# Layer 2's weights quantised and stored beside the convolution, and the first pair's layer 1 put between the weight chunks

## The reference, cut to what matters

```python
x = x + tanh(g_xattn[0]) * long_conv(ctx, ctx, layernorm(x), ssm_kernel, D, 8)
x = x + tanh(g_ffn[0]) * ffn(layernorm(x), ln_w, ln_b, W1, b1, W2, b2)

# long_conv, per head of 8 rows (64 heads, 1024 steps, batch 8)
kv  = einsum('bhil,bhjl->bijhl', k, v)                # k = v = ctx
y   = irfft(rfft(kv, 2L) * rfft(ssm_kernel, 2L))[:L]  # a causal convolution
out = einsum('bijhl,bhil->bjhl', y + kv * D, q)       # q = layernorm(x)

# ffn, on 4096 rows of 1024; hidden width 4096
h = bf16(layernorm(bf16(x)) * ln_w + ln_b)
h = bf16(mx_quant(h) @ mx_quant(W1).T + b1)
h = bf16(gelu(h))
h = bf16(mx_quant(h) @ mx_quant(W2).T + b2)
return bf16(bf16(x) + h)
# mx_quant: per block of 32 along the contraction, a power of two from the block's
# largest magnitude; round(x / scale), clipped to -128..127, times scale
```

## Time and profile before

| what | value |
|---|---|
| median of 3 runs | 2108.7 us (2106.93 to 2108.92) |
| the profiled execution | 2109.22 us |
| its span in the profile | 2107.4 us |
| PE busy | 1936.4 us (92%) |
| DVE busy | 1713.9 us (81%) |
| POOL busy | 915.4 us (43%) |
| ACT busy | 736.8 us (35%) |
| mixer block | about 0 to 1027 us |
| preparation of the weights | about 1027 to 1180 us |
| groups of tiles | about 1180 to 2107 us |

### The profile page before, as it was taken

One profiled execution on the slowest core, in us unless ns is written; L12 is line 12 of the kernel. 1 busy time (PEld: TensorE's weight loads), 2 busy tenths in 40 slices (PEclk: granted clock), 3 DMA queues, 4 the chain that ended last, 5 costly groups with the idle time before them and its releaser, 6 DMA issues.

```text
span 2107.4 us, 29465 instructions
## 1 busy us (share of the span) xinstructions
PE 1936.4 (92%) x11776; PEld 1493.9 (71%) x11776; DVE 1713.9 (81%) x2091; ACT 736.8 (35%) x1028; POOL 915.4 (43%) x1036
## 2 busy tenths in 40 slices
PE   6999999999999999999232579999999999999998
PEld 5888888888888888888231456666666666666663
DVE  6888788888888878887799888888888898888844
ACT  3222222222222222222141444444444444545440
POOL 4888888888888888888501000000000000000000
PEclk9999999999999999999655789999999999999999
DMA  5445445444544544542568201111111111111111
GB/s 196 147 163 183 151 156 176 163 143 170 172 149 155 182 159 153 171 153 98 188 213 280 78 21 61 61 61 45 55 53 60 61 61 41 51 61 61 41 41 70
DMA packets 61160, 247.62 MB, mean 117 GB/s; under 512 B 7200, under 2 KB 7200, under 8 KB 52832
## 3 DMA queue, kind: packets, MB, share of 16 engines
q1 hardware_dynamic: 61024, 245.74, 34.0%
HBM read 211.57 MB, written 34.14 MB: 117 GB/s over the span
## 4 chain that ended last, share of the span: by engine, by line
PE 43%; DVE 7%; issue 1%; DMA 0%; ACT 0%; POOL 0%; DVEq 0%; POOLq 0%; ACTq 0%
PE acc_ps L670 21%; PE l_ps L655 21%; DVE arena L915 2%; DVE f_o_res L915 2%; DVE w_T L930 1%; DVE arena L930 1%; PE tr_ps L633 1%; DMA arena<-in_w 0%; DVE f_stats L782 0%; DVE f_stats L781 0%; DVE arena L881 0%; DVE arena L891 0%; DVE f_amax_x L826 0%; DVE f_o_res L920 0%; DVE arena L920 0%
## 5 line engine op out<-in xcount | busy, mean ns | idle before, releaser
L217 PE MATMUL y_ps<-kk_hi,slab 128*128 128x512 f32 (+8 forms) x3072 | 870.6, 366 | 5.3 <-DMA slab<-taps_scratch 5.3
L217 PEld LDWEIGHTS y_ps<-kk_hi,slab 128*128 128x128 f32 x3072 | 557.7, 188 | 101.5 <-DMA slab<-taps_scratch 5.7
L217 PE MATMUL y_ps<-kk_lo,slab 128*128 128x512 f32 (+8 forms) x1536 | 561.9, 366 | 0.0
L655 PE MATMUL l_ps<-f_xq_T,w_T 128*128 128x256 bf16 x4096 | 457.7, 275 | 68.4 <-ACT arena L735 66.1
L655 PEld LDWEIGHTS l_ps<-f_xq_T,w_T 128*128 128x128 bf16 x4096 | 403.6, 99 | 123.2 <-ACT arena L735 66.7
L670 PE MATMUL acc_ps<-w_T,arena 128*128 128x512 bf16 x2048 | 449.0, 379 | 0.0
L670 PEld LDWEIGHTS acc_ps<-w_T,arena 128*128 128x128 bf16 x2048 | 198.8, 98 | 232.2
L991 POOL TENSOR_TENSOR f_rstd<-f_var_eps,f_neg_half 128x1 f32<-128x1 f32 x32 | 21.8, 682 | 741.9 <-DVE f_var_eps L794 741.9
L217 PEld LDWEIGHTS y_ps<-kk_lo,slab 128*128 128x128 f32 x1536 | 289.8, 189 | 47.5
L735 ACT ACTIVATE arena<-l_ps,f_b 128x256 bf16<-128x256 f32 x512 | 213.7, 471 | 279.8 <-PE l_ps L655 221.9
L453 POOL TENSOR_TENSOR lsum<-lower 128x240 f32<-128x240 f32 (+1 forms) x128 | 254.8, 1991 | 122.8 <-DVE lower L359 122.8
(11 more groups left out here) (101 smaller groups left out, 1954.1 us busy)
## 6 DMA issues: line engine op xcount, KB each, us to landing
slab<-taps_scratch SPq DMA_DIRECT2D x128, 512.0 KB, 4.4
arena<-in_w_m SPq DMA_DIRECT2D x32, 1024.0 KB, 6.9
arena<-x_scratch SPq DMA_DIRECT2D x64, 512.0 KB, 3.9
arena<-in_w SPq DMA_DIRECT2D x32, 1024.0 KB, 4.9
k_ext<-in_ctx_e SPq DMA_DIRECT2D x64, 384.0 KB, 3.0
x_tile<-in_x_t SPq DMA_DIRECT2D x32, 512.0 KB, 4.7
x_scratch<-x SPq DMA_DIRECT2D x32, 512.0 KB, 2.9
out_t<-arena SPq DMA_DIRECT2D x32, 512.0 KB, 2.6
```

The costliest lines, as they stand in the source:

```text
L217: mm = nc.tensor.matmul(y_ps[:, y_base + begin:y_base + end], slab[s][:, half, d * P:(d + 1) * P], kk_part[s][:, begin - d * PAIR:end - d ...
L655: mm = nc.tensor.matmul(l1_ps[bank % L1_BANKS][:, a, :], w1_T[:, k, col:col + P], xq_T[:, k, :], start=(k == 0), stop=(k == L // P - 1))
```

## The change

W2 gets its own layout (`w2_t`), a scratch tensor in HBM (`w2_q`, 16 chunks of 512 KB in bf16), and is quantised in the mixer block. There DVE takes the weight maxima on each of the first 32 heads (one a head, not one in two), makes all scales on head 32, and from head 32 on runs `layer2_ints` on each even head and `layer2_clip` and `layer2_quant` on each odd one. SP loads a maxima chunk on each of the first heads, and in the second half loads a chunk of W2 and stores a quantised one in each tile. In the feed-forward block the preparation has only W1's 16 chunks; SP loads the finished W2 after them. Tiles 0 and 1 are prepared before chunk 0 is finished, and PE runs bank j-1 of the first group's layer 1 after it has turned chunk j; ACT adds the biases and applies gelu in the same loop, DVE takes two of the four peaks and the statistics of tiles 2 and 3 in it. The wait quoted above is gone, since `hidden[0]` no longer lies in buffers of the raw weights (two of them are in `w2_T` now). The scales of W1 are made in half the width.

```diff
@@ mixer_block, sync
+            def load_w2(j):
+                if j >= 2:
+                    sp.wait_ge(w2_stored, 16 * (j - 1))
+                sp.dma_start(w2_raw[j % 2], w2_t[j]).then_inc(w2_loaded, 16)
+            def store_w2(j):
+                sp.wait_ge(w2_quant, j + 1)
+                sp.dma_start(w2_q[j], w2_raw[j % 2][:, 0:L].bitcast(BF16)).then_inc(w2_stored, 16)
...
-                    if t + 1 < tiles:
-                        sp.wait_ge(w_max_ready, t)
-                        load_w(t + 1)
+                if 1 <= h < tiles - 1:
+                    sp.wait_ge(w_max_ready, h)
+                    load_w(h + 1)
+                if h in (tiles - 2, tiles - 1):
+                    load_w2(h - (tiles - 2))
+                if t > half:
+                    if h % TILE_HEADS == 0:
+                        store_w2(t - half - 1)
+                    elif t + 1 < tiles:
+                        load_w2(t - half + 1)
...
             first_loads(sp)
+            store_w2(tiles - half - 1)
             store_x1(tiles - 1)
+            sp.wait_ge(w2_stored, 16 * (tiles - half))
@@ mixer_block, vector
+            def layer2_ints(j):
+                dve.wait_ge(w2_loaded, 16 * (j + 1))
+                if j == 0:
+                    dve.wait_ge(w_inv_ready, 2)
+                else:
+                    dve.wait_ge(w2_quant, j)
+                nc.vector.tensor_tensor(w2_int.rearrange("p (c o) -> p c o", o=L), w2_raw[j % 2].rearrange("p (c o) -> p c o", o=L),
+                                        view(w_inv, L, [(0, 2), (1, L)]), ALU.mult).then_inc(w2_ints, 1)
+            def layer2_clip(j):
+                dve.wait_ge(w2_ints, j + 1)
+                nc.vector.tensor_scalar(w2_int, w2_int, 127.0, None, ALU.min).then_inc(w2_clipped, 1)
+            def layer2_quant(j):
+                w2_scale_twice = view(w2_scale, 0, [(0, 2), (1, L)])
+                dve.wait_ge(w2_clipped, j + 1)
+                nc.vector.tensor_tensor(w2_raw[j % 2][:, 0:L].bitcast(BF16).rearrange("p (c o) -> p c o", o=L),
+                                        w2_int.rearrange("p (c o) -> p c o", o=L),
+                                        w2_scale_twice, ALU.mult).then_inc(w2_quant, 1)
...
-                if h % TILE_HEADS == 1:
-                    weight_maxima(t)
+                if h < tiles:
+                    weight_maxima(h)
+                if h == tiles:
+                    weight_scales()
+                if t >= half:
+                    if h % TILE_HEADS == 0:
+                        layer2_ints(t - half)
+                    else:
+                        layer2_clip(t - half)
+                        layer2_quant(t - half)
             times_q(heads - 1, 1)
-            weight_scales()
             residual(tiles - 1)
@@ ffn_block, sync
-            for j in range(2, 2 * n1):
-                if W_BUFS <= j < n1 + W_BUFS:
+            for j in range(2, n1):
+                if j >= W_BUFS:
                     sp.wait_ge(turned, 2 * (j - W_BUFS + 1))
...
+            for j in range(n1):
+                if j >= 12 and j % 2 == 0:
+                    sp.wait_ge(turned, 2 * (n1 - 1 + (j - 12) // 2))
+                load_layer2(j)
+            sp.wait_ge(quant_ready, n1)
@@ ffn_block, tensor (layer1 now takes a group and one bank)
+                if g == 0:
+                    pe.wait_ge(kept, 2 * (b + 1))
...
+            for t in range(GROUP):
+                turn_input(t)
             for j in range(n1):
                 turn_weights(j)
-                if j == 4:
-                    turn_input(0)
-                if j == 8:
-                    turn_input(1)
-            pe.wait_ge(kept, 2 * n1)
+                if j >= 1:
+                    layer1(0, j - 1)
+            layer1(0, n1 - 1)
@@ ffn_block, scalar
-                    if g == 0:
-                        act.wait_ge(quant_ready, 2 * n1)
...
             for j in range(n1):
                 keep_w1(j)
+                if j >= 2:
+                    add_bias(0, j - 2)
+                if j == 8:
+                    first_norm(2)
+                    first_norm(3)
+                if j in (6, 10, 14):
+                    gelu(0, (j - 6) // 4)
@@ ffn_block, vector
-            for j in range(2 * n1):
+            weight_ints(0)
+            for t in range(GROUP):
+                second_statistics(t)
+            weight_clip(0)
+            for t in range(GROUP):
+                weigh_input(t)
+                quantise_input(t)
+            weight_quant(0)
+            for j in range(1, n1):
                 weight_ints(j)
-                if j >= 1:
+                if j >= 2:
                     weight_quant(j - 1)
                 weight_clip(j)
...
+                if j in (11, 12):
+                    second_statistics(j - 9)
+                if j in (9, 13):
+                    peak(0, (j - 9) // 4)
```

More of the change, by code:

```diff
@@ L60, in wait_if_positive, with mixer_block @@
         eng.wait_ge(semaphore, count)
-def mixer_block(nc, x_t, ctx_e, taps_in, skip_in, g_x, scratch, x1_t, w_m, w_raw, w_inv, first_loads, tiles):
+def mixer_block(nc, x_t, ctx_e, taps_in, skip_in, g_x, scratch, x1_t, w_m, w_raw, w_inv, w2_t, w2_raw, w2_int, w2_q,
+                first_loads, tiles):
     heads = tiles * TILE_HEADS
     row = LB * PAIR
+    half = tiles // 2
     stretches = [(max(end - 512, 0), end) for end in range(row, 0, -512)]
@@ L479, in raw_weights, with ffn_block @@
     return arena[:, (X_LOADS + 1 + 2 * i) * L:(X_LOADS + 3 + 2 * i) * L]
[L482 to L487 removed]
+def ffn_block(nc, x1_t, ln_w, ln_b, w1_t, w2_q, b2_b, arena, x1_loaded, w_loaded, b1, b2, g_f, out_t, tiles):
     half = HID // 2
@@ L510, in ffn_block @@
         xfin = arena[:, X_LOADS * L:(X_LOADS + 1) * L]
-        w = [raw_weights(arena, i) for i in range(W_BUFS)]
+        w = [raw_weights(arena, 2), raw_weights(arena, 3)]
+        w += [w2_T[:, 24 + 4 * i:28 + 4 * i, :].rearrange("p c o -> p (c o)").bitcast(F32) for i in range(2)]
         hidden_base = (X_LOADS + 1) * L
@@ L644, in turn_weights, with layer1 @@
                     mm.then_inc(turned, 1)
-            def layer1(g):
-                pe.wait_ge(input_kept, GROUP * (g + 1))
-                for b in range(banks):
-                    bank = banks * g + b
-                    if bank >= L1_BANKS:
-                        pe.wait_ge(biased, bank - L1_BANKS + 1)
-                    for a in range(2):
-                        col = (2 * b + a) * P
-                        for k in range(L // P):
-                            mm = nc.tensor.matmul(l1_ps[bank % L1_BANKS][:, a, :], w1_T[:, k, col:col + P], xq_T[:, k, :],
-                                                  start=(k == 0), stop=(k == L // P - 1))
-                    mm.then_inc(l1_ready, 1)
+            def layer1(g, b):
+                bank = banks * g + b
+                if b == 0:
+                    pe.wait_ge(input_kept, GROUP * (g + 1))
+                if g == 0:
+                    pe.wait_ge(kept, 2 * (b + 1))
+                if bank >= L1_BANKS:
+                    pe.wait_ge(biased, bank - L1_BANKS + 1)
+                for a in range(2):
+                    col = (2 * b + a) * P
+                    for k in range(L // P):
+                        mm = nc.tensor.matmul(l1_ps[bank % L1_BANKS][:, a, :], w1_T[:, k, col:col + P], xq_T[:, k, :],
+                                              start=(k == 0), stop=(k == L // P - 1))
+                mm.then_inc(l1_ready, 1)
             def layer2(t, part):
@@ L674, in layer2 @@
                     mm.then_inc(l2_ready, 1)
+            for t in range(GROUP):
+                turn_input(t)
             for j in range(n1):
                 turn_weights(j)
-                if j == 4:
-                    turn_input(0)
-                if j == 8:
-                    turn_input(1)
-            pe.wait_ge(kept, 2 * n1)
+                if j >= 1:
+                    layer1(0, j - 1)
+            layer1(0, n1 - 1)
             for g in range(groups + 1):
-                if g < groups:
-                    layer1(g)
+                if 1 <= g < groups:
+                    for b in range(banks):
+                        layer1(g, b)
                 for s in range(GROUP):
@@ L745, in _ @@
             first_norm(1)
+            for t in range(GROUP):
+                keep_input(t)
+            act.wait_ge(const_loaded, 16 * 4)
+            nc.scalar.activation(gate_tanh[:], gate[:], ACT.Tanh).then_inc(gate_ready, 1)
             for j in range(n1):
                 keep_w1(j)
-                if j == 6:
-                    keep_input(0)
-                if j == 10:
-                    keep_input(1)
-            act.wait_ge(const_loaded, 16 * 4)
-            nc.scalar.activation(gate_tanh[:], gate[:], ACT.Tanh).then_inc(gate_ready, 1)
-            first_norm(2)
-            first_norm(3)
+                if j >= 2:
[5 more added lines that the diff above has]
+                    gelu(0, (j - 6) // 4)
```

(9 more changed lines are left out.)

68 lines of the change are left out of this document (33 added, 35 removed).

## The result

The changed kernel takes 2045.5 us (median of 4 runs, 2044.03 to 2045.63) against 2107.8 (4 runs, 2106.86 to 2108.92): a ratio of 0.970, 95% interval 0.969 to 0.972. The forecast was 2055 with 2040 to 2073, so the time lies inside the range and 10 us under the forecast. The profiled execution took 2045.5, with a span of 2043.7; it is set against the 2109.2 of before.

What follows compares the result with a forecast made beforehand. PE was taken to pace the convolution and DVE the preparation up to PE's restart. From 2109.2, the feed-forward block gave -65.2 and the convolution +11.2, making 2055.2; predicted 2055, range 2040 to 2073.

Steps and rivals of the forecast that it cites:

- Block, -68.5 + 3.3: Feed-forward block: 68.5 us saved by removed chunks, waits and overlapped layer 1, less 3.3 for lags, net -65.2.
- The +3.3 for lags: Preparation: PE lagging behind DVE, and loads waiting for late turns, cost 3.3 us; bounds 0 and +11.
- rival 2: Preparation: PE stays at half clock, 8 us over the forecast, 2063 in all; chance 0.16.
- that is all the moved layer 1 brings: Preparation: layer 1 between the chunks saves only the 4.2 us of gelu waits, since DVE was the path.
- Head 32: Convolution's middle: scales and first ints delay the products to 10.0 after head 32, so PE pauses 3.8 us.
- POOL as the pace by 0.64 a pair: Convolution's second half: POOL needs 31.55 a pair against PE's 30.91, 9.0 us over 14 pairs.
- the lock term: Convolution's second half: DVE's low_half and W2 steps hold POOL off for 8.75 us a pair of heads.
- The working's other estimate: Convolution's second half: POOL's busy share of 26.8 a pair plus 4.18 exceeds PE's pace by only 0.07.
- rival 1: Convolution's second half: POOL has room, so the convolution costs only +3, 2047 in all; chance 0.22.
- Rival 3: Convolution: DVE waits for POOL's running adds, 1.0 a pair beyond the forecast, +15, 2070; chance 0.17.
- an L453 of 2.9 in the second half: Convolution's second half: this POOL add was forecast at 4 to 5 us on ints heads; 2.9 would refute the POOL account.
- -2.2 for the scales and +1.8 for clip and quant in head 63: Convolution's end: POOL's last part loses the 2.2 us weight_scales caused; clip and quant add 1.8.

Runs made afterwards that it cites:

- the first part alone: Changed kernel with layer 1 of the first two tiles put back after W1's chunks, W2 still quantised beside the convolution: 2056.12 us.

## Why the prediction was right, and where not

- **Which stage gives and which takes**: right. The feed-forward block gave 69.1, and the convolution took 5.2.
- **Block, -68.5 + 3.3**: measured -69.1. W1's chunks with what is moved between them take 96.3 on DVE (1032.74 to 1129.05; "about 97"), and PE restarts 37.7 later. The +3.3 for lags was not needed. PE's granted clock, which the prediction wanted above 0.8, was 0.74 on the mean of the stage, but 0.91 from 1070 to 1110 and 0.83 from there to 1130; at full clock a bank takes 1.91 and a turn 1.06, together less than DVE's 3.94 a chunk, so PE waits for DVE, and DVE waited for no load. The worry that the clock would stay low (rival 2) came from the 0.53 of a stretch in which PE had little to do.
- **"-4.2: that is all the moved layer 1 brings"**: the number is right as the difference between the two kernels, and wrong as the worth of that part. With W2 gone the waits for gelu would have been 11.0 (the experiment with layer 1 after the chunks), so the first part alone would not have brought its full 63: the block takes 145.4 there, 57.8 less than before. The parts are not additive, and the sum hid it.
- **Head 32**: the burst was forecast as 3.8 of pause with the products 10.0 after the head's end; 4.14 and 10.2 were measured. The term was mis-sized all the same, 7.07 in place of 3.8: the restart behind a pause (0.25) and the clock at its lower level behind it (2.7) were left out, though the earlier trace rows had a slow start in the 6.69.
- **Convolution, POOL as the pace by 0.64 a pair**: this step failed, and with it 8.2 of the +11.2 (the prediction's own bound without it is +3). What was mis-sized is the lock term. POOL's own 22.8 a pair was right. For the locks the sum has 8.75; by the rows above they are (2.82 - 0.70) + (3.06 - 1.02) on the even head and (3.01 - 0.70) + (1.48 - 1.02) + (1.69 - 0.70) on the odd one, 7.9. That makes 30.7, under PE's 30.91, and the 0.20 a pair in which POOL waits is the rest. The busy time agrees: 390.0 - 347.4 = 42.6 us more in 12.9 pairs, 3.3 a pair in place of 4.18. The steps held POOL off for less than their length, since at the seam between two of them one of POOL's adds goes first and DVE waits. The working's other estimate, from the busy share (0.07), has the same 4.18 and leaves out the 0.57 a pair ahead of the adds of L520; two errors that partly cancel (by it POOL would need 30.98; it needs 30.7). So rival 1 (POOL has room, 2047) is what happened, with the block 3.9 better and the convolution 2.2 worse than in its sum. That its number came out within 2 us is partly luck.
- **Rival 3's mechanism** is real: DVE waits for POOL's adds, 0.5 to 0.7 on each of three steps. It costs nothing in the pairs, since DVE still had some 0.9 of idle time ahead of `times_q(h,0)` (24.4 in 26 heads) and the burst 0.75 of room. The clip run twice shows how near it was: 0.69 us more on odd heads costs some 15.
- **The signs that the prediction named**: an L453 of 2.9 in the second half was to make its account of POOL wrong, and that is what came: the same add (L508 now) takes 2.82 and 3.01, 2.89 on the mean, and never the 4 to 5 forecast. A `low_half` longer than 2.55 came only slightly (2.54 and 2.59).
- **End of the convolution, -2.2 for the scales and +1.8 for clip and quant in head 63**: measured -2.3 in all. POOL's last part runs from 1019.12 to 1025.66, 6.54, with nothing beside it. The +1.8 did not come: without W2's steps the end is as long.

The errors, 6.0 in the convolution and 3.9 in the block, have the same sign and make the 10. Of the 6.0, 8.2 are POOL's pairs and 1.5 the end (the bound of +3, with 3.8 of pause in it, leaves -0.8 for what came as -2.3), less 3.3 at head 32 and 0.5 at the start.

## What to carry to other kernels

When two engines both look nearly full, don't ask which has the larger sum. Follow the longest burst between two hand-overs (here `low_half` to the last product) and compare it with what PE has in hand. Locks summed from single rows came out too high (4.18 a pair, 3.3 measured), and a busy share leaves out the short fixed steps between instructions (0.57 a pair): where the two estimates lie on either side of the pace, as here, neither decides. Work that must stand in such a burst goes in small steps over many rounds, since one round with too much pays for its pause and again for the clock behind it. What feeds the next round's first stage (here two tiles' statistics, 3.5 us) goes ahead of a long chain that nobody awaits.

## What the runs showed of the hardware

- A pause of 2.03 us of a PE that had been busy for 500 us already brings the granted clock down behind it; 1.5 us are lost by it, and 1.3 to 2.7 behind 4.14 (six executions). Pauses of 0.74 and 1.25 on every pair of heads did not (PE's clock averages 1.00 from 550 to 985 in both), nor did one of 1.81 at 576.74 in the run with the ints twice (1.00 in the 4.3 us behind it).
- DVE instructions of the kinds that hold POOL off are held off by POOL in turn, whatever their size: 8 columns took 0.67 to 0.94 beside an add, and 0.16 the one time that there was none. A one-input reduction of 576 columns beside the same adds took 0.75, and the step behind it was shorter by 0.67.
- Two executions of the same kernel differ by 1.1 in the gap behind one pause and by 0.5 in the start of the convolution, at medians 1.5 apart.
